# Layer 0 of a two-layer graph network: the destination one-hot moved to ScalarE, two operands moved to PSUM, exponentials and weighing put directly behind the shift

## The reference

```
layer 0:  xl = x @ W_l ; xr = x @ W_r                       (4 heads x 32)
          e    = sum_c leaky_relu(xl[src] + xr[dst]) * att   per edge and head (self loops too)
          p    = exp(e - max over the edges of dst)
          out  = segment_sum(p * xl[src], dst) / segment_sum(p, dst) + bias + x
          x1   = layernorm(x + layernorm(out) * gamma + beta)
layer 1:  neigh = segment_sum(x1[src] + edge_attr, dst)
          out  = layernorm(x1 + mlp(2 * x1 + neigh))
```

## Time and profile before

| | |
|---|---|
| median of 3 runs | 4612.28 us (4607.57 to 4612.98) |
| the profiled execution | 4611.55 us, its span 4609.7 us |
| busy: PE, PE weight loads | 3464.4 us (75%), 2604.3 us (56%) |
| busy: DVE, ACT, POOL | 2131.5 us (46%), 577.0 us (13%), 3181.3 us (69%) |
| DMA | 512.32 MB, mean 111 GB/s |

### The profile page before, as it was taken

How to read it: one execution, slowest core, us unless ns; L and a number is a source line. 1 busy time by engine, 2 the same in 40 slices (tenths; PEclk the granted TensorE clock), 3 DMA queues, 4 the chain that set the end, 5 groups by cost and what they waited for, 6 DMA issues and landing times. The chain is left out here.

```text
span 4609.7 us, 71384 instructions
## 1 busy us (share of the span) xinstructions
PE 3464.4 (75%) x18612; PEld 2604.3 (56%) x18613; DVE 2131.5 (46%) x7034; ACT 577.0 (13%) x1586; POOL 3181.3 (69%) x3295
## 2 busy tenths in 40 slices
PE   6899999999999999999786555555555555555559
PEld 4555655655655655555465555555555555555557
DVE  7566676667766766766475111111111111111117
ACT  3111111111111111111054000000000000000005
POOL 3777777777777777777333777777777777777750
PEclk9899999999999999999788777777777777777779
DMA  6643433343343343344255333333333333333323
GB/s 180 171 114 108 114 114 109 114 114 111 113 114 112 111 113 113 110 114 114 76 138 100 103 107 103 108 104 107 105 105 107 103 107 103 108 103 107 103 71 114
DMA packets 460317, 512.32 MB, mean 111 GB/s; under 512 B 179918, under 2 KB 360014, under 8 KB 460278
## 3 DMA queue, kind: packets, MB, share of 16 engines
q1 hardware_dynamic: 277526, 262.17, 19.4%
q0 software_dynamic: 100352, 208.93, 16.5%
q10 hardware_dynamic: 82400, 40.77, 3.1%
HBM read 464.25 MB, written 47.30 MB: 111 GB/s over the span
## 5 line engine op out<-in xcount | busy, mean ns | idle before, releaser
L497 POOL DMA_INDIRECT rows<-xl_table,src_idx x1568 | 1586.4, 1012 | 532.6 <-issue 517.4
L1072 POOL DMA_INDIRECT rows<-x_table,src_idx x1568 | 1480.8, 944 | 504.3 <-issue 477.4
L528 PE MATMUL ph<-node_of,xr_win 128*128 128x512 f32 x784 | 752.9, 1095 | 1.3 <-issue 1.3
L1086 PE MATMUL pA<-edge_of,dst_row 128*128 128x128 f32 x1568 | 327.7, 394 | 472.3 <-DMA rows<-x_table,src_idx 389.0
L1086 PE MATMUL pT<-node_of,dst_row 128*128 128x128 f32 x1568 | 324.1, 391 | 437.1 <-DMA rows<-x_table,src_idx 388.3
L1086 PEld LDWEIGHTS pA<-edge_of,dst_row 128*128 128x128 f32 x1568 | 305.9, 299 | 488.3 <-issue 486.9
L1086 PEld LDWEIGHTS pT<-node_of,dst_row 128*128 128x128 f32 x1568 | 302.4, 296 | 452.9 <-issue 451.3
L565 PE MATMUL pA<-wmsg,edge_of 128*128 128x136 f32 x3168 | 426.1, 288 | 7.1 <-DVE edge_of L782 6.6
L565 PEld LDWEIGHTS pA<-wmsg,edge_of 128*128 128x128 f32 x3168 | 385.8, 192 | 11.4 <-issue 8.0
L554 PE MATMUL pT<-att_heads,relu_h 128*128 128x56 f32 x3136 | 390.9, 278 | 1.3 <-DVE shifted L811 1.3
L640 ACT ACTIVATE relu_h<-ph 128x512 f32<-128x512 f32 x392 | 234.2, 597 | 1185.8 <-PE ph L528 1185.8
(11 more groups left out here) (168 smaller groups left out, 4154.1 us busy)
## 6 DMA issues: line engine op xcount, KB each, us to landing
dst_row<-in_dst SPq DMA_DIRECT2D x196, 513.0 KB
dst_row<-in_edge_attr SPq DMA_DIRECT2D x195, 512.0 KB, 3.6
rows<-xl_table,src_idx POOLq DMA_INDIRECT x1568
rows<-x_table,src_idx POOLq DMA_INDIRECT x1568
sums_table<-win ACTq DMA_DIRECT2D x198, 68.0 KB
rows<-in_x SPq DMA_DIRECT2D x100, 128.0 KB, 2.3
xr_win<-xr_table SPq DMA_DIRECT2D x196, 64.0 KB
sums_table<-win ACTq DMA_DIRECT2D x1, 6868.0 KB
```

Of the source, the lines that this page charges most:

```text
L497: pool.indirect_dma_start(rows[s][:, t, :], None, xl_table[:, :], bass.IndirectOffsetOnAxis(ap=src_idx[s][:, t:t + 1], axis=0))\
L528: return [pe.matmul(h[:, k:k + 4, :], xr_of[:, :], by_tile[:, k:k + 4, :], start=False, stop=stop) for k in range(0, T, 4)]
L1072: pool.indirect_dma_start(rows[s][:, t, 0:D], None, x1_table[:, :], bass.IndirectOffsetOnAxis(ap=src_idx[s][:, t:t + 1], axis=0))\
L1086: ins = pe.matmul(bank, m[:, t, :], one_hot[:, t, :], start=(k == 0 and t == 0), stop=(k == 1 and t == T - 1))
```

## The change

The one-hot of the destinations, `node_of`, is made by ACT with two activations, 1 - |id - node| clipped at zero, and no longer by one comparison on DVE. It is written tile by tile (element `t*128 + p`), so that the product L528 reads it without a step, while ACT's first activation writes with a step of 128 elements. Of the former `node_one_hot`, DVE keeps the one-element addition (`first_of`). The row of node numbers against which `edge_one_hot` compares, and the weights that `weigh` multiplies by, are now in PSUM; the weights are made by a third exponential there. The linear part of the logits is added by DVE (into SBUF) instead of the PE product L556, and the carried sum is added on DVE to the first message instead of the PE product L579.

The order changes too. PE: `sources(g+1)` comes ahead of the wait for run(g). ACT: the exponentials come ahead of `keep(g-1)`, and `node_one_hot(g+2)` comes last. DVE: `carry(g-1)` stands where `weigh(g-1)` stood; `first_of(g+2)` and `prepare(g+1)` come ahead of `shift(g)`, and `weigh(g)` directly behind it.

```diff
-        fwd, run = sb("fwd", [P, H * T]), sb("run", [P, H * T])
+        logits, fwd, run = (sb(n, [P, H * T]) for n in ("logits", "fwd", "run"))
         step_pen = sb("step_pen", [P, H * T + 1])
-        pen_first, pen_last, is_last = (sb(n, [P, T]) for n in ("pen_first", "pen_last", "is_last"))
+        pen_first, pen_last, is_last = ([sb(f"{n}{s}", [P, T]) for s in range(2)] for n in ("pen_first", "pen_last", "is_last"))
...
+        def in_tiles(t):
+
+            return t.rearrange("n (t p) -> n p t", t=T)
...
-        logit = logit_all[:, 0:H * T]
+        products, logit = logit_all[:, 0:H * T], logits[:, :]
+        weights = pT1[:, 2 * P:2 * P + H * T].rearrange("p (h t) -> p h t", h=H)
+        near_row = pT1[:, 3 * P:4 * P]
...
                     def product(xr_of, one_hot, stop):
-                        by_tile = one_hot.rearrange("n (p t) -> n t p", t=T)
+                        by_tile = one_hot.rearrange("n (t p) -> n t p", t=T)
...
-                        pe.matmul(out_t[:, t, :], relu_h[0][:, t, :], att_heads[:, :], start=(t == 0), stop=False)
-                    linear = rows[g.c % U][:, :, D:DW].rearrange("p t h -> p h t")
-                    pe.matmul(by_head(logit), ident[:, :], linear, start=False, stop=True).then_inc(S("logit_ready"), 1)
+                        ins = pe.matmul(out_t[:, t, :], relu_h[0][:, t, :], att_heads[:, :], start=(t == 0), stop=(t == T - 1))
+                    ins.then_inc(S("products_ready"), 1)
...
                     pe.wait_ge(S("edge_of_made"), g.times(1, 1))
-                    visit(0)
-                    pe.matmul(pA[0][:, 0:WC], first_row[0:1, :], carried[0:1, :], start=False, stop=True)\
-                      .then_inc(S("summed"), 1)
+                    visit(0).then_inc(S("summed"), 1)
...
+                    if beyond:
+                        sources(g + 1)
                     if more:
                         pe.wait_ge(S("run_ready"), g.times(1, 1))
                         run_h = by_head(run)
                         pe.transpose(pT1[0:H, 0:P], run_h[:, :, T - 1], ident[:, :])
                         pe.transpose(pT1[0:H, P:2 * P], run_h[:, :, 0], ident[:, :]).then_inc(S("ends_across"), 1)
                     if beyond:
-                        sources(g + 1)
                         targets(g + 1, near(g + 1))
...
+                def node_one_hot(g):
+
+                    s, of = g.c % U, node_of[g.c % 2][:, :]
+                    act.wait_ge(S(f"row_in0{s}"), g.use(16, 16))
+                    act.wait_ge(S("first_made"), g.times(1, 1))
+                    if g.at_least(2):
+                        act.wait_ge(S("h_ready"), g.times(2, -2))
+                    ids = dst_row[s][:, 1:1 + G].rearrange("n (p t) -> n p t", t=T)
+                    act.activation(in_tiles(of), ids, ACT.Abs, scale=-1.0, bias=first_node[:, s:s + 1])\
+                       .then_inc(S("distance_made"), 1)
+                    act.wait_ge(S("distance_made"), g.times(1, 1))
+                    act.activation(of, of, ACT.Relu, scale=-1.0, bias=one[:, :]).then_inc(S("node_of_made"), 1)
...
                     if not g.at_least(1):
+                        node_one_hot(g)
+                        node_one_hot(g + 1)
                         relu(g)
                     if not (g.j is None and g.c + 1 >= groups):
                         relu(g + 1)
-                    if g.at_least(1):
-                        keep(near(g + -1))
                     if not (g.j is None and g.c >= groups):
                         act.wait_ge(S("shifted_ready"), g.times(1, 1))
                         heads = wmsg[g.c % 2][:, :, 0:H * HC].rearrange("p t (h k) -> p t h k", k=HC)
+                        act.activation(weights, shifted[:, :, 0:T], ACT.Exp)
                         act.activation(heads[:, :, :, C], shifted[:, :, 0:T].rearrange("p h t -> p t h"), ACT.Exp)
                         act.activation(r_exp[:, :], shifted[:, :, T], ACT.Exp).then_inc(S("weights_ready"), 1)
+                    if g.at_least(1):
+                        keep(near(g + -1))
+                    if not (g.j is None and g.c + 2 >= groups):
+                        node_one_hot(g + 2)
...
+                def first_of(g):
                     v.wait_ge(S(f"row_in0{s}"), g.use(16, 16))
-                    hide.at(g.times(HIDE_LINKS))
-                    hide.link(v.tensor_tensor(first, node_id[:, 0:1], dst_row[s][:, 1:2], ALU.add))
-                    if g.at_least(2):
-                        v.wait_ge(S("h_ready"), g.times(2, -2))
-                    v.tensor_scalar(node_of[g.c % 2][:, :], ids, first, None, ALU.is_equal)\
-                     .then_inc(S("node_of_made"), 1)
+                    v.tensor_tensor(first_node[:, s:s + 1], node_id[:, 0:1], dst_row[s][:, 1:2], ALU.add)\
+                     .then_inc(S("first_made"), 1)
...
 
-                    soft.at(g.times(SOFT_LINKS), PREPARE_LINKS)
-                    v.wait_ge(S("logit_ready"), g.times(1, 1))
+                    soft.at(g.times(SOFT_LINKS))
+                    v.wait_ge(S("products_ready"), g.times(1, 1))
+                    linear = rows[g.c % U][:, :, D:DW].rearrange("p t h -> p h t")
+                    soft.link(v.tensor_tensor(by_head(logit), by_head(products), linear, ALU.add))
...
                     v.wait_ge(S("weights_ready"), g.times(1, 1))
                     v.tensor_tensor(heads[:, :, :, 0:C], rows[s][:, :, 0:D].rearrange("p t (h c) -> p t h c", h=H),
-                                    heads[:, :, :, C:HC].to_broadcast([P, T, H, C]), ALU.mult)\
+                                    weights.rearrange("p h t -> p t h").unsqueeze(3).to_broadcast([P, T, H, C]), ALU.mult)\
                      .then_inc(S(f"rows_free0{s}"), 1)
+
+                def carry(g):
+
                     if g.at_least(1):
 
                         v.wait_ge(S("picked"), g.times(1, 0))
                         by = lambda t: t[0:1, 0:H * HC].rearrange("o (h k) -> o h k", k=HC)
+                        first_message = wmsg[g.c % 2][0:1, 0, 0:H * HC]
                         v.tensor_tensor(by(carried), by(pick), r_exp[0:1, :].unsqueeze(2).to_broadcast([1, H, HC]),
-                                        ALU.mult)
+                                        ALU.mult).then_inc(S("carried_made"), 1)
+                        v.wait_ge(S("carried_made"), g.times(1, 1))
+                        v.tensor_tensor(first_message, first_message, carried[:, 0:H * HC], ALU.add)
...
                     one_hot = lambda k: v.tensor_tensor(edge_of[k][:, :, :], dst_rel[:, :].unsqueeze(2).to_broadcast([P, T, P]),
-                                                        node_row[:, :].unsqueeze(1).to_broadcast([P, T, P]), ALU.is_equal)
+                                                        near_row.unsqueeze(1).to_broadcast([P, T, P]), ALU.is_equal)
...
                     last = g + -1
                     more = not (g.j is None and g.c >= groups)
                     if not g.at_least(1):
-                        node_one_hot(g)
+                        first_of(g)
+                        first_of(g + 1)
                         further_one_hots(g, near(g))
-                        node_one_hot(g + 1)
                         prepare(g)
                     if more:
                         maxima(g)
                     if not (g.j is None and g.c + 1 >= groups):
                         further_one_hots(g + 1, near(g + 1))
                     if g.at_least(1):
-                        weigh(last)
+                        carry(last)
                     if more:
                         across(g)
                     if g.at_least(1):
                         edge_one_hot(last, near(last))
+                    if not (g.j is None and g.c + 2 >= groups):
+                        first_of(g + 2)
+                    if not (g.j is None and g.c + 1 >= groups):
+                        prepare(g + 1)
                     if more:
                         shift(g)
-                    if not (g.j is None and g.c + 2 >= groups):
-                        node_one_hot(g + 2)
-                    if not (g.j is None and g.c + 1 >= groups):
-                        prepare(g + 1)
+                        weigh(g)
```

39 lines of the change are left out of this document (20 added, 19 removed).

## The result

| | before | after |
|---|---|---|
| median of the program | 4611.39 us (4607.57 to 4612.98, 4 runs) | 4786.16 us (4784.16 to 4786.39, 4 runs) |
| ratio to before | | 1.0382, 95% interval 1.0369 to 1.0395 |
| distance of two groups in layer 0 | 10.84 us | 11.76 us |

The profiled execution of the changed kernel took 4786.39 us, with a span of 4784.6. The forecast was 4676 us with a range of 4540 to 4900. The place of the loss is as forecast; of the 175 us that were lost, the forecast had 64.

The account below looks back on a forecast made before the run. PE's queue was taken to bound the kernel before; after the change a ring of waits, ACT's 4.33 plus DVE's 6.84 = 11.17 us a group against 10.84, adds 195 x 0.33 = 64 us to 4611.55: 4676 us, range 4540 to 4900.

Parts of the forecast that it names:

- first activation: ACT's first of two passes making the one-hot, writing with a step; forecast 1.15 us, step priced at zero.
- ACT's part: ACT's stretch from the end of DVE's shift to the finished one-hot; forecast 4.33 us a group.
- DVE's part: DVE's stretch from the one-hot's end to the end of the next shift; forecast 6.84 us a group.
- The ring: Layer 0's waits from shift over ACT's one-hot to next shift; claimed to set the group distance, 11.17 us against 10.84.
- the stepped write: ACT's first activation writing with a step of 128 elements; extra cost taken as zero, upper end 1.10 us.
- the slow-write rival: ACT's first activation pays 1.10 us more for its step: 12.27 us a group, 4890 us; chance 0.25.
- The direction: Whole program slower, by 0.33 us a group or 64 us; chance of slower 0.72.
- The loss at the loop's end: Time lost where DVE's loop goes round, 0.46 us for each group in the mean; claimed to be covered.
- PE without the step: PE's product L528 reading without a step: 2.0 us instead of 3.83; PE busy 7.8 us a group, about 70%.
- The gathers: POOL's gathers: 0.95 us each, POOL waiting about 1 us per group for source indices.
- The rival in which the gathers set the pace: Ring shorter than it looks, so POOL's gathers bound layer 0: 4520 us, floor 4477; chance 0.20.
- The two rules that were weighed: Skill rules: accesses to new 16-byte SBUF lines pay a penalty; DVE instructions with two SBUF inputs block GpSimd SBUF reads.

Follow-up runs that it names:

- a1: Changed kernel with the destination one-hot in edge order again: ACT writes without a step, PE reads with a step of 8; 4612.24 us, ratio 1.0006.
- d1: Changed kernel with only the step of ACT's first write removed, PE's reads unchanged, output not the reference's; 4620.14 us, ratio 1.0015.
- a4: Changed kernel with DVE's `prepare` of group g+1 behind the weighing again instead of ahead of the shift; 4553.9 us, ratio 0.9878.
- c2: Changed kernel with the diffs of a1 and c1 together: one-hot first on ACT, operands in edge order; 4455.55 us, ratio 0.9662.
- a2: Changed kernel with the one-hot made on DVE behind the weighing, operands in edge order; 4512.58 us, ratio 0.979.
- c1: Changed kernel with the one-hot first in ACT's step and DVE making `first_of(g+2)` directly behind the scans; 4492.25 us, ratio 0.9738.
- d2: Changed kernel with ACT's second activation also stepping by 128 elements, in reading and writing; 4966.05 us, ratio 1.0768.
- c3: Changed kernel with the weighing and the edge comparison reading their operands from SBUF again instead of PSUM; 4796.98 us, ratio 1.0400.
- c4: Kernel a2 with the weighing and the edge comparison reading their operands from SBUF again instead of PSUM; 4571.32 us, ratio 0.9911.
- a3: Changed kernel with ACT's one-hot of group g+2 moved ahead of the exponentials of group g; 4507.58 us, ratio 0.978.

## Why the prediction was too small, and right in direction by luck

The circle in the means of 168 groups of the changed kernel, against the terms of the sum:

| term | forecast, us | measured, us |
|---|---|---|
| link, three exponentials | 0.04 + 0.53 | 0.04 + 0.47 |
| gap, `keep` with its store, waits ahead of the one-hot | 0.05 + 1.21 + 0.10 | 1.20 |
| **first activation** | **1.15** | **2.07** |
| link, second activation | 0.10 + 1.15 | 0.03 + 1.15 |
| ACT's part | 4.33 | 4.96 |
| wait and loop to L741, next instruction | 0.54 + 0.08 | 0.49 + 0.08 |
| carry | 0.53 | 0.53 |
| up to the end of the edges' one-hot | 2.26 | 2.27 |
| wait and loop to L722, next instruction | 0.54 + 0.08 | 0.53 + 0.08 |
| `prepare`, link, shift | 1.62 + 0.04 + 1.15 | 1.61 + 0.04 + 1.16 |
| DVE's part | 6.84 | 6.79 |
| sum | 11.17 | 11.74 |

- **The ring, and that ACT and DVE turn by turn set the distance:** right. L741 waits where it was said to; DVE's part is off by 0.05 us. DVE's idle time ahead of it was to be 1.4 us and is 2.44, larger by about the first activation's excess.
- **The failed step is one term of the sum:** the stepped write, "I take zero, with 1.10 as the upper end". It costs 2.067 - 1.150 = 0.92 us. The forecast had the rows that pointed to it, named their per-element price, and set them aside because they were reads. With 0.92 the sum is 11.17 + 0.92 = 12.09, and 4676 + 195 x 0.92 = 4855 us; the remaining terms of ACT's part were 0.29 us too long and DVE's 0.05, together 66 us the other way. The two errors had opposite signs, and the slow-write rival (4890), which had the right mechanism, was too high for the same reason and by the 0.18 us between 1.10 and 0.92.
- **The direction was luck:** the forecast's 64 us were 0.33 us a group, made up of terms that turned out 0.34 us too long. With the first activation at the forecast's own 1.15 us the distance is 10.87 or 10.88 us against 10.84 before, and the time 4612 or 4620 us (a1, d1), where the forecast had 4676. All that was lost is the price that the forecast had set at zero.
- **ACT's other terms too long:** the waits ahead of the one-hot (0.10 by estimate) and the gap in front of `keep` do not show, and the link between the activations is 0.03, not 0.10. Each of these three estimates, which no row stood behind, was too long.
- **The loss at the loop's end is covered:** right. The distances of the four groups of a loop are 11.8, 11.7, 11.7 and 11.8 us. a4 shows that it comes back as soon as `prepare` fills the cover.
- **PE without the step:** right. L535 takes 1.98 us for four instructions, 2.0 forecast, against 3.83. It didn't help, since PE was no longer the bound: with the step back in PE and out of ACT (a1) the program is 174 us faster. PE is busy 74%, 70% forecast, that is 0.74 x 11.76 = 8.7 us a group against 7.8; in a4, where the transposes are slow in 2 groups only, it is 0.76 x 10.57 = 8.0, so most of the difference is groups at half the clock.
- **The gathers:** 0.953 us, 0.95 forecast, and POOL waits (802.1 - 486.1) / 196 = 1.6 us more per group than in c2, where nothing but the gathers sets the pace; 1 us was forecast, again by the longer circle. The rival in which the gathers set the pace did not happen here, but a2 and c2 turn it on by taking ACT off the ring, and c1 nearly does.
- **The two rules that were weighed:** ACT pays 0.90 ns more for each element with the step in a1 (2067 against 1150 ns for 1024), 0.85 in d2. The Trainium skill's lines of 16 bytes (SBUF — State Buffer, section Door 1: The DMA port swizzle) agree with this and so hold for ACT's writes as far as this one step of 512 bytes can tell; no run tries another step, so the length of the line is not tested. The forecast cited them against the change and gave them too little weight. The gather is 33 to 34 ns longer where DVE reads both operands from SBUF (c3, c4), and in c2 at 948 ns within 2 ns of the 946 of its own layer 1. The Trainium skill (SBUF — State Buffer, section Who interferes with whom) names that effect, and the runs agree in its sign.

## What to carry to other kernels

When an idle engine is given work, draw the circle of waits that it joins before counting busy time: the 0.92 us of the stepped write cost the program 166 to 174 us where they stand between the wait that starts the circle and the one that closes it, and with the one-hot moved ahead of the exponentials (a3) the program is faster than before although the step is still there. A stepped access doesn't become free when it is moved to another engine (0.90 ns an element on PE, 0.90 on ACT), so it belongs where it is off that circle (here PE's reads, though PE is the busiest). And if two engines show one price for an access pattern, that price, not zero, is the likeliest for the third.

## What the hardware showed that was not expected

- ACT writing 1024 fp32 elements per partition with a step of 512 bytes takes 2.067 us, without 1.150. Stepping in both reading and writing (d2, in place) takes 2.021 us: the prices don't add.
- DVE pays for such a write too, but less: in the loop for further windows, which runs twice in the program, its comparison of 1024 elements takes 1320 ns in the changed kernel and 1318 in d1, where it writes with a step of 512 bytes, and 752 in a1, where it doesn't: 0.55 ns an element.
- The same eight transposes on PE take 1.09 or 1.97 us from one group to the next, that is at 2.4 or 1.2 GHz. They are slow in 116 of 196 groups of c1 (PE busy 84%, granted clock 0.89), in 96 of the changed kernel (74%, 0.92), and in 7 of c2 (94%, 0.99), but in only 2 of a4 (76%, 0.97). The busy share alone doesn't tell which kernel gets the slow groups.
- One operand of each of DVE's two large instructions moved from SBUF to PSUM shortens another engine's instruction, the mean gather, by 33 to 34 ns, and DVE's own by 5 ns.
